# A transformer block on one core: keys stored with their differences, later transposes of the maxima, the three-way split spread out, and square roots taken as a power on GpSimd

## What is computed

```python
x = x + attn_a(_layernorm(x))    # 16 heads of 8, full softmax over 1024 keys, exact to float32
x = x + ffn(_layernorm(x))       # 3 layers with weights +-1
x = x + attn_b(_layernorm(x))    # 8 heads of 16; window of 64 earlier tokens, the 32 nearest kept
x = x + ffn(_layernorm(x))
```

```python
# attn_a
scores = jnp.einsum('bqhd,bkhd->bhqk', q, k)
probs = jax.nn.softmax(scores, axis=-1)
out = jnp.einsum('bhqk,bkhd->bqhd', probs, v)
# attn_b, for each head
wsq = diff * diff * metric
dist = jnp.sqrt(wsq.sum(-1) + 1e-08)
neg, loc = jax.lax.top_k(-dist, 32)      # over the 64 tokens of the window
topd = -neg
infl = jnp.exp(-topd)
infl = infl / (infl.sum(-1, keepdims=True) + 1e-08)
```

## Time and profile before

| what | value |
|---|---|
| median of 3 runs | 3201.6 us (3197.55 to 3203.15) |
| the profiled execution's own time | 3204.65 us |
| its span, first to last instruction | 3202.8 us |
| mean granted TensorE clock | 0.909 |
| busy: PE | 2629.4 us (82%) |
| busy: PE weight loads | 1200.3 us (37%) |
| busy: ACT | 2331.6 us (73%) |
| busy: DVE | 2128.0 us (66%) |
| busy: POOL | 618.0 us (19%) |

### The profile page before, as it was taken

The page is one execution under the profiler, slowest core; times in us unless marked ns, Lnnn a source line. Parts: engine busy times, 40 slices in busy tenths (PEclk is TensorE's granted clock), DMA queues, the critical chain, the costliest instruction groups (busy, mean ns, idle before and its releaser), DMA issues.

```text
span 3202.8 us, 73054 instructions
## 1 busy us (share of the span) xinstructions
PE 2629.4 (82%) x22579; PEld 1200.3 (37%) x22579; DVE 2128.0 (66%) x10282; ACT 2331.6 (73%) x3225; POOL 618.0 (19%) x797
## 2 busy tenths in 40 slices
PE   5878778889788888888879888898978888887666
PEld 2212243344333443334433344333433344333444
DVE  5701668846776668856689466885677666892595
ACT  4697569967698667976689666996669866795433
POOL 2010013101131112401132011311123111221232
PEclk6599689999899998999989998999989998999888
DMA  2011001000010000100000000000001000000000
GB/s 80 14 36 31 2 1 38 28 15 6 9 35 29 11 6 9 48 22 8 2 33 29 17 9 9 32 28 16 5 9 39 29 10 2 9 2 1 1 8 8
DMA packets 60585, 58.20 MB, mean 18 GB/s; under 512 B 15218, under 2 KB 41524, under 8 KB 60196
## 3 DMA queue, kind: packets, MB, share of 16 engines
q1 hardware_dynamic: 59952, 52.95, 5.3%
q10 hardware_dynamic: 244, 0.39, 0.0%
HBM read 35.66 MB, written 17.56 MB: 17 GB/s over the span
## 4 chain that ended last, share of the span: by engine, by line
PE 40%; ACT 24%; issue 20%; DVE 10%; POOL 4%; SPq 2%; ACTq 0%; DMA 0%; DVEq 0%; POOLq 0%
PE banks L756 37%; ACT PT L1097 11%; ACT pq L1084 3%; POOL Aop L735 2%; DVE pq L1217 2%; PE banks L763 1%; ACT h L1109 1%; ACT xn L1046 1%; DVE xn L1434 1%; DVE h L1437 1%; ACT hparts L1108 1%; ACT h L1156 1%; POOL qkf L709 1%; PE banks L988 1%; SPq L520 1%
## 5 line engine op out<-in xcount | busy, mean ns | idle before, releaser
L1097 ACT ACTIVATE PT<-banks 128x1024 f32<-128x1024 f32 x1024 | 996.4, 1035 | 47.9 <-PE banks L756 38.9
L1217 DVE CUSTOM_DVE_ANT_0 pq<-pq,banks 128x512 f32<-128x512 f32 x1024 | 660.2, 685 | 269.6 <-ACT pq L1084 241.7
L1084 ACT ACTIVATE pq<-banks 128x1024 f32<-128x1024 f32 x512 | 523.5, 1022 | 337.3 <-PE banks L756 328.4
L756 PE MATMUL banks<-K,Q 48*128 48x512 bf16 x3072 | 494.8, 435 | 87.3 <-ACT pq L1084 65.2
L756 PE MATMUL banks<-PT,Vg 128*32 128x512 f32 x4096 | 560.2, 620 | 2.0 <-ACT PT L1097 2.0
L756 PE MATMUL banks<-Q,K 51*128 51x512 bf16 x2048 | 397.6, 396 | 168.0 <-ACT PT L1097 158.8
L719 POOL TENSOR_TENSOR hparts<-h,hparts 128x512 fp32r<-128x512 f32 x112 | 140.3, 1272 | 1152.1 <-ACT h L1109 1152.0
L1434 DVE MATCH_REPLACE8 xn<-h,xn 128x96 f32<-128x96 f32 x1536 | 352.6, 243 | 0.0
L756 PEld LDWEIGHTS banks<-Q,K 51*128 51x128 bf16 x2048 | 108.8, 93 | 590.4 <-issue 560.3
L756 PE MATMUL banks<-hparts,W 128*128 128x512 f32 x1024 | 301.9, 423 | 27.6 <-ACT h L1109 21.7
L756 PEld LDWEIGHTS banks<-K,Q 48*128 48x128 bf16 x3072 | 127.6, 100 | 399.4 <-issue 341.4
(11 more groups left out here) (200 smaller groups left out, 3412.7 us busy)
## 6 DMA issues: line engine op xcount, KB each, us to landing
scratch_qk<-pq SPq DMA_DIRECT2D x24, 512.0 KB, 2.7
qkf<-in_hidden_states SPq DMA_DIRECT2D x16, 512.0 KB, 3.9
Q<-scratch_qk SPq DMA_DIRECT2D x126, 48.0 KB
K<-scratch_qk SPq DMA_DIRECT2D x126, 48.0 KB
Q<-scratch_qk SPq DMA_DIRECT2D x126, 32.0 KB
K<-scratch_qk SPq DMA_DIRECT2D x126, 32.0 KB
out<-xr SPq DMA_DIRECT2D x14, 256.0 KB, 2.3
K<-scratch_qk SPq DMA_DIRECT2D x126, 16.0 KB
```

The costliest lines, as they stand in the source:

```text
L756: return pe.matmul(o, l, r, start=start, stop=stop)
L1084: act.activation(cut(g), ring_pair if work is TURN0 and g % 2 else pair[0], ACT.Relu).then_inc(diff_out.sem, 1)
L1097: act.activation(PT[:, at:at + 2, :], pair[g % ESLOTS], ACT.Exp, scale=1.0 if i % 8 < 4 else -1.0).then_inc(probs.sem, 1)
L1217: dve.tensor_tensor_reduce(r, r, pair[1 + g % 2][:, par, :], 1.0, -3.0e38, ALU.subtract, ALU.max, mred[:, par, i, qt:qt + 1]).then_inc(max ...
```

## The change

It has four parts. (1) POOL adds near and negated far keys to a third block of 512 columns, `kd`; it is split into three parts like the keys and stored behind them (`KT` = 1536 columns), so the difference of a group is one pair of matmuls in place of two. `Vg` loses its padding (9 columns a head), which makes the room. (2) The transpose of quad n's maxima stands at group 16(n+1)+2.1, and that of the last quad at 0.02 of phase two. (3) The split is spread over stage `qk` and five stages `split` behind it; in it are two more roundings on ACT and three more operations on POOL, all 128x512; SP writes the parts with six DMAs, once the last split stage has come. (4) The Ln and the Exp of the square root leave ACT. POOL does them behind the mask: a multiplication by -1 and a power with exponent 0.5, both 128x768, in stage `dev`; 1e-8 moves into `outside`.

```diff
-SLOTS_H = [(1.0, [(s, 0)]) for s in ("x", "ln", "lnr", "lnf", "lnn", "lnTa", "qk")]
+SLOTS_H = [(1.0, [(s, 0)]) for s in ("x", "ln", "lnr", "lnf", "lnn", "lnTa", "qk")] + [(1.0, [("split", i)]) for i in range(5)]
...
+MTURNS = [(((n + 1) * QGROUPS + 2.1) / GROUPS, [("a", "mturn", n)]) for n in range(NQUAD - 1)], [(0.02, [("a", "mturn", NQUAD - 1)])]
...
-    one, two = [FIRST_V, MAXES, MROWS], [exp_slots()]
+    one, two = [FIRST_V, MAXES, MROWS, MTURNS[0]], [exp_slots(), MTURNS[1]]
...
-        K = sb("K", [P, NQUAD, 2, T], BF16)
-        Vg = sb("Vg", [P, NU, NH, VW])
+
+        K = sb("K", [P, NQUAD, 2, KT], BF16)
+        Vg = sb("Vg", [P, NU, NH, HD + 1])
...
+        kd = xT[:, HALF:T]
...
-                        for part, last in enumerate((act_a.at(b, 2), act_a.at(b, 4), pool_a.at(b, 4))):
+                        for part, last in enumerate((act_a.at(b, 3), act_a.at(b, 6), pool_a.at(b, 6))):
                             sp.wait_ge(*last)
                             pass_waits(sp)
-                            sp.dma_start(scratch_qk.rearrange("(w s) c t -> s c w t", w=2)[part],
-                                         pq[:, :, :].rearrange("c (w s) t -> c s w t", w=2)[:, part]).then_inc(split_out[part].sem, 16)
+                            sp.dma_start(scratch_q[part], q_parts[:, part, :]).then_inc(split_out[part].sem, 16)
+                            sp.dma_start(scratch_k[part], k_parts[:, part, :]).then_inc(split_out[part].sem, 16)
...
+                        pool.wait_ge(*R.moved(c, use["qk", 0] + 2))
+                        pool.wait_ge(*R.moved(c, use["qk", 0] + 3))
+                        pool.tensor_tensor(kd, qkf[:, 1, 0:HALF], qkf[:, 1, HALF:T], ALU.add).then_inc(kd_a.sem, 1)
                         for w in range(2):
-
                             pool.wait_ge(*act_a.at(b, w + 1))
-                            pool.tensor_tensor(qkf[:, w, :], qkf[:, w, :], pq[:, 3 * w, :], ALU.subtract).then_inc(pool_a.sem, 1)
...
+                            pool.tensor_tensor(qkf[:, w, :], qkf[:, w, :], parts_of(w, 0), ALU.subtract).then_inc(pool_a.sem, 1)
+                    if (stage, n) == ("split", 0):
+                        pool.wait_ge(*act_a.at(b, 3))
+                        pool.tensor_tensor(kd, kd, parts_of(2, 0), ALU.subtract).then_inc(pool_a.sem, 1)
+                    if stage == "split" and 1 <= n <= 3:
+                        w = n - 1
+                        pool.wait_ge(*act_a.at(b, w + 4))
+                        pool.tensor_tensor(parts_of(w, 2), whole(w), parts_of(w, 1), ALU.subtract).then_inc(pool_a.sem, 1)
...
                         pool.tensor_tensor(d, d, outside[:, :].unsqueeze(1).broadcast_to([P, SH, WW]),
                                            ALU.add).then_inc(d_pool.sem, 1)
+                        e = E[:, n % 2, :, :]
+                        pool.wait_ge(*d_pool.at(b, n + 1))
+                        if n >= 2:
+                            pool.wait_ge(*R.moved(c, use["wt", n - 2] + 1))
+                        pass_waits(pool)
+                        pool.tensor_scalar(e, d, -1.0, None, ALU.mult).then_inc(e_steps.sem, 1)
+                        pool.wait_ge(*e_steps.at(b, n + 1))
+                        pool.tensor_tensor(e, e, root[:, 0:1].unsqueeze(2).broadcast_to([P, SH, WW]), ALU.pow).then_inc(e_root.sem, 1)
...
-                        near, far = slice(0, HALF), slice(HALF, T)
-                        for dst, keys, start, stop in ((diff, near, True, False), (diff, far, False, True),
-                                                       (pair[1 + g % 2], far, True, True)):
+                        for dst, keys in ((diff, slice(T, KT)), (pair[1 + g % 2], slice(HALF, T))):
...
-                            ins = mm(ov_bank[i // 8][VW * j:VW * j + VW, :], Vg[:, i % 8, 4 * n + 2 * (j // 2) + j % 2, :],
+                            ins = mm(ov_bank[i // 8][VW * j:VW * j + HD + 1, :], Vg[:, i % 8, 4 * n + 2 * (j // 2) + j % 2, :],
...
+                    if (stage, n) == ("split", 0):
+                        act.wait_ge(*kd_a.at(b, 1))
+                        act.activation(parts_of(2, 0), kd, ACT.Identity).then_inc(act_a.sem, 1)
+                    if stage == "split" and 1 <= n <= 3:
+                        w = n - 1
+                        act.wait_ge(*pool_a.at(b, w + 1))
+                        act.activation(parts_of(w, 1), whole(w), ACT.Identity).then_inc(act_a.sem, 1)
...
-                        if r == 0:
-                            act.wait_ge(*d_pool.at(b, n + 1))
-                            act.activation(e, D[:, n % 2, :, :], ACT.Ln, scale=-1.0, bias=eps8[:, :]).then_inc(e_steps.sem, 1)
-                        if r == 1:
-                            act.wait_ge(*e_steps.at(b, 2 * n + 1))
-                            act.activation(e, e, ACT.Exp, scale=0.5).then_inc(e_steps.sem, 1)
                         if r == 2:
-                            act.wait_ge(*e_steps.at(b, 2 * n + 2))
+                            act.wait_ge(*e_root.at(b, n + 1))
                             act.activation(e, e, ACT.Exp, scale=-1.0).then_inc(e_act.sem, 1)
```

More of the change, by code:

```diff
@@ L35 @@
 MROW = len(QPART) * HD
+KT = T + HALF
 VW = 32
@@ L185, in phases @@
     order = merged(*one) + merged(*two)
+    assert not ahead or order.index(("h", "split", 4)) < order.index(("h", "load", 0))
     if twice:
@@ L203, in numbered @@
     return said, use, k
-HEAD = [("h", s, 0) for s in ("ln", "weights", "lnr", "lnf", "lnn", "lnTa", "qk")] + [("h", "load", 0), ("h", "tables", 0)]
-HEAD += [("h", "load", n) for n in range(1, NQUAD)]
+HEAD = [("h", s, 0) for s in ("ln", "weights", "lnr", "lnf", "lnn", "lnTa", "qk")] + [("h", "split", i) for i in range(5)]
+HEAD += [("h", "load", 0), ("h", "tables", 0)] + [("h", "load", n) for n in range(1, NQUAD)]
 TAIL_SPANS = dict(o=(0.000, 0.090), p=(0.075, 0.380), t=(0.380, 1.000), q=(0.380, 0.700), z=(0.723, 0.915))
@@ L339, in hybrid_block_kernel @@
         ones1 = sb("ones1", [1, 1])
-        eps8 = sb("eps8", [P, 1])
+        root = sb("root", [P, 1])
         qkf = sb("qkf", [P, 2, T])
@@ L456, in hybrid_block_kernel @@
         xb_a = count("bias_added", 1)
-        act_a = count("part_rounded", 4)
-        pool_a = count("part_left", 4)
-        split_out = [count(f"split_out{part}", 1, 16) for part in range(PARTS)]
+        act_a = count("part_rounded", 6)
+        pool_a = count("part_left", 6)
+        kd_a = count("keys_subtracted", 1)
+        split_out = [count(f"split_out{part}", 2, 16) for part in range(PARTS)]
         quad_in = [count(f"quad{n}_in", 1, 24 * 16) for n in range(NQUAD)]
@@ L592, in go @@
                         if work is not TURN7:
-                            sp.wait_ge(*split_out[2].at(b, 2))
+                            sp.wait_ge(*split_out[2].at(b + 1, 2))
                             pass_waits(sp)
                         sp.dma_start(xres[:, :, :], x_t[b]).then_inc(res_in.sem, 16)
-                    if stage == "qk":
+                    if (stage, n) == ("split", 4):
                         for n in range(NQUAD):
@@ L671, in _ @@
             link(pool.memset(ones3[:, HALF:T], -1.0))
-            link(pool.memset(Vg[:, :, :, :], 0.0))
             link(pool.memset(Vg[:, :, :, HD:HD + 1], 1.0))
@@ L675, in _ @@
             link(pool.memset(ones1[:, :], 1.0))
-            link(pool.memset(eps8[:, :], 1e-8))
             select(identb[:, :], [[-1, P]], 0, 1, 1.0, ALU.not_equal)
@@ L682, in _ @@
                 select(t[:, :], [[step_, width]], lo + SE - 1, -1, 0.0)
-            link(pool.memset(outside[:, :], 0.0))
+            link(pool.memset(outside[:, :], -1e-8))
+            link(pool.memset(root[:, :], 0.5))
             link(pool.memset(offself[:, :, :], 1.0))
@@ L830, in go @@
                                 pe.wait_ge(*R.moved(c, use["v", 0] + 1))
-                            if g > 1 and g % QGROUPS == 1:
+                            if g > QGROUPS and g % QGROUPS == 3:
                                 pe.wait_ge(*R.moved(c, use["mturn", n - 1]))
@@ L847, in go @@
                                 rows_ = slice(64 * par, 64 * par + MROW)
-                                ins = mm(dst[:, par, :], Q[rows_, n, i, P * qt:P * qt + P], K[rows_, n, i, keys], start, stop)
-                            if stop:
-                                ins.then_inc((diff_in if dst is diff else far_in).sem, 1)
+                                ins = mm(dst[:, par, :], Q[rows_, n, i, P * qt:P * qt + P], K[rows_, n, i, keys])
+                            ins.then_inc((diff_in if dst is diff else far_in).sem, 1)
                     if stage == "mturn":
@@ L1051, in go @@
                     if stage == "lnT":
+                        if work is not LAST and n == ((0, 0) if work is TURN1 else (2, 0)):
+                            act.wait_ge(*pool_a.at(c, 6))
                         evict(c, k, xT_[:, HALF * n[1]:HALF * n[1] + HALF], R.bank(k)[:, :])
@@ L1072, in go @@
```

(7 more changed lines are left out.)

51 lines of the change are left out of this document (28 added, 23 removed).

## The result

The changed kernel takes **10684.3 us** (median of 4 runs, 10678.8 to 10685.5), the kernel before in the same comparison 3202.35. The ratio is 3.337, with an interval from 3.331 to 3.343. The forecast was 3048 us, with a range to 3200. It was wrong in sign and by far in size; the rival that the power overruns its budget came true, with a power longer than that rival priced.

A forecast was written before the change was run, and what follows sets the result against it. PE was taken to bound phase one, ACT phase two with PE close behind, waits between PE and DVE the tail. Terms -79 - 15 - 12 - 20 + 21 + 6 - 61 + 6 = -154 from 3204.65 gave 3051, forecast 3048 us, range 2970 to 3200.

The forecast's parts named there:

- the rival that the power overruns its budget: POOL in Part 4: past 10 us for multiplication and power, 64 us lost per further us; 3496 at 17; chance 0.18 slower.
- the power's price in Part 4: POOL's power of 128x768 behind the mask: 8 us, with the multiplication 9.5; ends 3 and 17 for both.
- ten such steps: Power on POOL as logarithm, product and exponential, in ten register steps an element: 8 us.
- the upper end of twenty: Power on POOL priced as twenty steps: 15.3 us, or 17 with the multiplication.
- budget of 10 us: POOL in a unit of phase two: 10 us of added work fit before PE waits for `Aop`.
- -79 - 15 - 12 - 20 + 6: Part 1 in seven turns, Part 1 in turn 0, inner transposes, turns of the phases, longer head, in us.
- the +21 of Part 3: Split's added POOL operations in phase two meeting the power, ACT waiting: 3 us a turn, +21 us (0 to +50).
- Part 1, phase one: A saved pair of difference matmuls in each of 64 groups: 11.3 us of 14.1 in seven turns, -79 us.
- inner transposes: Part 2 inside phase one: half of PE's 3.3 us of idling at three transposes saved, -12 us over seven turns.
- Turn 0: With fewer difference matmuls DVE bounds turn 0: 100 us become about 85, -15 us (bounds -8 and -16).
- Head: Before PE's first scores nothing covers POOL's 3.4 us and the longer load of K: +6 us (+3 to +10).
- ACT's relief: Phase two without ACT's Ln and Exp: 8.7 us of 13.0 gained in seven turns, -61 us (bounds -30 and -91).

The follow-up runs named there:

- dose4: The changed kernel with four more multiplications of 128x768, each with a wait, in the power's place on POOL, square root left out: 3455.2 us.
- no_root: The changed kernel with the square root left out and nothing in its place; ACT takes exp of D directly, POOL gets no added work: 3062.0 us.
- sqrt_back: The changed kernel with the square root back on ACT as Ln and Exp, so Parts 1 to 3 alone: 3112.3 us, ratio to before 0.9711.

## Why the prediction was wrong, point by point

**The term that failed is the power's price in Part 4.** It was put at 8 us, with 17 as the upper end for both operations; it is 122.7. The step was "as ten such steps it is 768 x 10.3 ns": the number of steps was a guess with no row behind it, and so was the upper end of twenty. The multiplication was put at 1.5 us and took 2.14, so the way from rows to a simple operation was out by under a half; the power is a routine of another kind, 160 ns a column in place of 10.3. The bound from above should have been called open, and with it the range and the chances: 0.18 for the overrun was far too little for a price that no row held from above.

The Trainium skill's sentence pointed the right way. By its chain of dependent operations (GPSIMD Engine Reference, "Performance pitfalls for Q7 kernels") an estimated 25 us came out, already a loss of hundreds of us. The measured 122.7 us is five times that; whether the chain is longer than ten links or the routine is no such chain, no run here shows. As the only price from above it deserved more weight in the chances.

**How an overrun is paid was right.** The rival said 64 us of time for each us of the power. Between dose4, with 11.4 us of POOL's work between mask and operand, and the change, with 124.9, it is (10684 - 3455) / 113.5 = 63.7. By the rival's own formula 124.9 us give 3048 + 64 x 114.9 = 10402, within 3% of the result.

**The budget of 10 us was misread.** From dose4 down that slope to no_root's 3062 us is 6.2 us, which leaves a budget of 5.2, and not even 2.14 us are free. The wrong step was to take one unit in the middle of the phase for all eight. The first unit of each phase has 0.7 us before the change, and none after Part 2; in the units of the split POOL's queue is fuller; and POOL itself waits 1.55 us for the free half of E in the unit shown above, which the sum left out. With the assumed power of 8 us, about 10.3 for both, the kernel would have been an estimated 3455 - 1.1 x 63.7 = 3385 us by that slope, slower than before even so.

**Parts 1 to 3, forecast and measured.** Together the forecast's terms for them are -79 - 15 - 12 - 20 + 6, and 1.1 us on ACT in seven turns, some -112 us (the +21 of Part 3 was for meeting the power); measured -90.
- Part 1, phase one: 188.7 to 177.8 us in sqrt_back's turn 3. With 1.7 us of it for the inner transposes that is 9.2 a turn, forecast 11.3. PE's time went as priced: 254 matmuls in place of 380, with 9.8 us of idling in front of them, not 8.7, in the changed kernel:

```profile
L788 PE MATMUL banks<-K,Q 48*128 48x512 bf16 x254 | 43.1, 405 | 9.8 <-ACT pq L1119 7.0 <-DVE mred L1246 2.1
```

- Turn 0: 89.9 us, forecast 85. DVE bounds it as foreseen, busy 81.4 of 89.9.
- Part 2: 34 us alone and 43 with Part 1; forecast 32 and turn 0's share. The first scores still wait 3.91 us for the last cut; that wait was said to be 2.5 us shorter than 5.46, and this is 1.5 shorter, with the 0.5 us between the transpose's start and the scores gone as well; of these 2 us, 1.77 are lost again to the wait for `Aop`.
- Head: PE's first scores wait for the load of K and phase one starts at 53.6 us in sqrt_back in place of 45.5, 8 us, forecast 6.
- ACT's relief: 50 us by no_root, forecast 61.

So Part 1's phases, Part 2 and ACT's relief were right within a fifth or so; turn 0 (10 us for 15) and the head (8 for 6) were out by a third, and the budget by half or more. The term that did not stand on rows decided the result. The version that beats both kernels is sqrt_back, Parts 1 to 3 without the power, at 0.9711 of the time before.

## What to carry to other kernels

An operation that no trace shows has no upper bound from rows of other operations; a pass that only adds says nothing of a routine that works out a power. Measure it by itself first, in a setup where it can hold up nobody, or else leave the range open on that side. And when work is put in front of an operand in a queue, read the slack in every unit of the ring, the first one above all, not in the one that looks typical.

## What was not expected of the hardware

- A power in float32 on GpSimd costs 0.160 us a column of 128 partitions, and the same with one partition: 128x768 122.7 us, where the addition of the same shape takes 1.82 and ScalarE's Ln and Exp together 1.77.
- While it runs, VectorE's operations with two inputs in SBUF are held if they start in its first microseconds. From DVE's timeline, the first beside the power that starts at 3773.56 above, the last beside one that starts 0.44 us before it:

```profile
3774.74 80.89 DVE L1481 TENSOR_TENSOR h<-h,sq 128x128 f32<-128x128 f32 x1
3855.67 0.29 DVE L1482 TENSOR_TENSOR h<-h,qtok 128x128 f32<-128x128 f32 x1
...
9541.65 122.24 DVE L1223 TENSOR_SCALAR ls<-mv 128x4 f32<-128x4 f32 x1
```

  In all 14 holds of two-input operations in turns 3 and 4 the hold ended 81.9 to 82.7 us after the power's start, two thirds of its length. Such operations in its last third ran at their usual time: L1482 above started 82.1 us into the power. Small operations with one input in SBUF were held to its very end, wherever they started: L1232 (8 columns) from 82.2 us in, L1223 (4 columns, in the tail) from 0.4, 1.4 and 89.3 us in. Operations reading PSUM (L1479, 0.29 us) weren't held. MAX8 and MATCH_REPLACE8 weren't either, but for two MATCH_REPLACE8 in the tail, each recorded beside a held L1223, that ended with it. The Trainium skill says that GpSimd shares its SBUF interfaces with VectorE, for instructions with two SBUF inputs or in a 2-port mode (GPSIMD Engine Reference, "Specifications"). The trace agrees on the two-input ones for two thirds of the power; whether the one-input ones ran in a 2-port mode it doesn't show. With the power cut to 96 columns there was no hold at all (0.295 us). Why 768 columns hold and 96 don't wasn't tried further.
